# Graph aggregation and routed experts on one core: every engine's turn reordered, and the last two of five epochs joined

## The reference, cut to what matters

```python
# x (12500, 256); src, dst (212500,) with dst sorted; edge_weight (212500,)
def gnn(features, src, dst, w, W, b):
    msgs = features[src] * w[:, None]
    agg = segment_sum(msgs, dst, 12500)
    return agg @ W.T + b
def ffn(xf, ...):                      # 8 experts, D 256, H 512
    probs = softmax(xf @ gate_w + gate_b)
    top2_vals, top2_idx = top_k(probs, 2)
    ...
    # per expert e: y = gelu(xf @ W1[e] + b1[e]) @ W2[e] + b2[e]; out += weight[e] * y
x = x + gnn(layernorm(x), src, dst, edge_weight, W, b)
out = x + ffn(layernorm(x), ...)
```

## Time and profile before

| | |
|---|---|
| median of 3 runs | 2977.66 us (2973.94 to 2983.93) |
| the profiled execution's own time | 2972.63 us |
| its span, first to last instruction | 2970.9 us |
| mean granted clock of PE | 0.869 of full speed |
| busy PE, DVE, ACT, POOL | 74%, 51%, 23%, 62% of the span |
| mean share of the 16 DMA engines | 222 GB/s moved; 41.1% for SP's queue, 27.6% for POOL's |
| gathers | from 3.0 to 2585.4 us |

### The profile page before, as it was taken

The page is one execution under the profiler, slowest core; times in us unless marked ns, Lnnn a source line. Parts: engine busy times, 40 slices in busy tenths (PEclk is TensorE's granted clock), DMA queues, the critical chain, the costliest instruction groups (busy, mean ns, idle before and its releaser), DMA issues.

```text
span 2970.9 us, 47965 instructions
## 1 busy us (share of the span) xinstructions
PE 2196.5 (74%) x11446; PEld 1714.3 (58%) x11447; DVE 1502.6 (51%) x6264; ACT 685.0 (23%) x1950; POOL 1830.6 (62%) x1912
## 2 busy tenths in 40 slices
PE   3666767877777889787787786897887687665585
PEld 2444444665565677565665565676666566554474
DVE  8865454354363554554554544545555363554122
ACT  3411111221221222221221222222222222222131
POOL 6666777767767667767677677675765655500121
PEclk8778879888898999898898898998998888886798
DMA  9654747658568578578698587595976867655674
GB/s 344 231 191 140 234 119 239 212 179 261 193 191 256 189 237 292 173 250 278 198 293 260 167 273 228 181 299 164 297 256 206 262 214 251 180 177 152 208 242 159
DMA packets 306367, 659.36 MB, mean 222 GB/s; under 512 B 61604, under 2 KB 198598, under 8 KB 290342
## 3 DMA queue, kind: packets, MB, share of 16 engines
q1 hardware_dynamic: 213686, 402.45, 41.1%
q0 software_dynamic: 90960, 248.50, 27.6%
q10 hardware_dynamic: 1440, 5.26, 0.5%
HBM read 552.90 MB, written 212.26 MB: 258 GB/s over the span
## 4 chain that ended last, share of the span: by engine, by line
PE 30%; DVE 16%; SPq 16%; POOL 14%; issue 12%; DMA 11%; ACT 1%; DVEq 0%; ACTq 0%; POOLq 0%
POOL rows L383 13%; PE bank L648 9%; SPq L511 9%; PE bank L728 7%; PE bank L741 7%; DMA slots<-stage 4%; SPq L348 3%; DMA w<-in_w 2%; PE bank L680 2%; DVE spread L1037 2%; DMA results<-y_sb,result_i 1%; PE bank L671 1%; DVE item_t L1210 1%; DMA xi<-slots 1%; PE bank L718 1%
## 5 line engine op out<-in xcount | busy, mean ns | idle before, releaser
L383 POOL DMA_INDIRECT rows<-xhat,src_t x1536 | 1476.3, 961 | 522.3 <-issue 460.3
L648 PE MATMUL bank<-rows,spread 128*80 128x256 f32 x3328 | 878.7, 424 | 152.8 <-issue 63.7
L648 PEld LDWEIGHTS bank<-rows,spread 128*80 128x80 f32 x3328 | 552.1, 170 | 423.5 <-issue 197.7
L410 POOL DMA_INDIRECT results<-y_sb,result_i x231 | 229.1, 992 | 520.7 <-DVE y_sb L1243 477.1
L728 PE MATMUL bank<-xiT,w 128*128 128x128 f32 x3696 | 479.2, 285 | 66.0 <-issue 39.0
L728 PEld LDWEIGHTS bank<-xiT,w 128*128 128x128 f32 x3696 | 462.1, 199 | 98.6 <-issue 52.9
L741 PE MATMUL bank<-w,hT 128*128 x1848 | 480.4, 406 | 14.9 <-issue 7.5
L1050 DVE TENSOR_TENSOR acc<-acc,bank 128x160 f32 x208 | 67.0, 322 | 669.9 <-PE bank L638 639.5
L741 PEld LDWEIGHTS bank<-w,hT 128*128 128x128 f32 x1848 | 361.5, 205 | 72.4 <-issue 24.8
L879 ACT ACTIVATE hT<-bank,b1T 128x128 f32<-128x128 f32 x924 | 264.3, 368 | 575.8 <-PE bank L728 572.4
L1037 DVE TENSOR_SCALAR spread<-iota_w,dst_rel,wgt 128x80 f32<-128x80 f32 x1536 | 379.3, 339 | 0.1
(11 more groups left out here) (170 smaller groups left out, 1720.1 us busy)
## 6 DMA issues: line engine op xcount, KB each, us to landing
w<-in_w SPq DMA_DIRECT2D x231, 512.0 KB
slots<-stage SPq DMA_DIRECT2D x784, 136.0 KB
xi<-slots SPq DMA_DIRECT2D x231, 136.0 KB, 4.0
stage<-sorted_x SPq DMA_DIRECT2D x98, 272.0 KB
got<-results SPq DMA_DIRECT2D x97, 256.0 KB
rows<-xhat,src_t POOLq DMA_INDIRECT x1536
x_t<-in_x SPq DMA_DIRECT2D x97, 128.0 KB, 3.1
x_d<-x_t SPq DMA_DIRECT2D x97, 128.0 KB
```

The costliest lines, as they stand in the source:

```text
L383: pool.indirect_dma_start(rows[q][:, c, :], None, x if g < RAW else xhat, bass.IndirectOffsetOnAxis(ap=src_t[:, g * CG + c:g * CG + c + 1] ...
L410: pool.indirect_dma_start(results, bass.IndirectOffsetOnAxis(ap=result_i[i % 2][:], axis=0), y_sb[i % 2][:], None).then_inc(y_out[i % 2], 16)
L648: done = nc.tensor.matmul(B_SUM[0:W, 0:D], spread[g % 2][:, c, :], rows[q][:, c, :], start=c == 0, stop=c == CG - 1)
```

## The change

The plan: a part's softmax, choosing and placing may follow in the turn after the last gate instead of one later, a tile's mask and sort stand in the same turn (after the turn of the place), its copy runs in the turn after it. Results are scattered two turns after their step while edges are gathered. Combined tiles are stored a turn later (`stores`). The last two epochs, of parts (4, 4) and (2, 2, 2), become one of (4, 4, 2, 2, 2): 224 items and 237 turns instead of 231 and 239.

The engines: PE does gate transposition and linear before the down product and sorts after the logits, its second half behind the sums; `rank` goes from the turn of the choosing to that of the placing. The sort gets a PSUM bank of its own, and the up product has one bank instead of two. DVE makes the mask first in a turn. ACT, and not SP, issues the stores of sorted tiles and of residual rows. SP stores outputs and loads items first and copies runs last. Rings: results 2 to 4 (`YB`), output buffers 2 to 6 (`CB`).

```diff
-EPOCH_SIZES = ((6, 8, 8, 8), (8, 8, 8, 8), (8, 6, 4, 4), (4, 4), (2, 2, 2))
+EPOCH_SIZES = ((6, 8, 8, 8), (8, 8, 8, 8), (8, 6, 4, 4), (4, 4, 2, 2, 2))
+YB = 4
+CB = 6
...
-            elif k not in soft_at and gate_at.get(end, tau) < tau:
+            elif k not in soft_at and gate_at.get(end, tau + 1) <= tau:
...
-        if turns:
-            t.sort, t.stage, t.runs = turns[-1].mask, turns[-1].sort, turns[-1].stage
-        if send_next < NT and place_at.get(PART_OF[send_next], tau + 1) <= tau:
-            t.mask = send_next
+        if send_next < NT and place_at.get(PART_OF[send_next], tau) < tau:
+            t.mask = t.sort = send_next
             send_next += 1
+        if turns and turns[-1].sort >= 0:
+            t.stage = turns[-1].sort
...
+        for back in turns if not busy else turns[:-1]:
+            t.results += [s[0] for s in back.steps if s[0] >= 0 and s[0] not in result_at]
         if turns:
-            t.results = [s[0] for s in turns[-1].steps if s[0] >= 0]
-            t.combines = turns[-1].fetches
+            t.combines, t.stores = turns[-1].fetches, turns[-1].combines
...
-        B_SUM, B_TURN, B_XI, B_H0, B_H1, B_Y, B_NODE, B_GATE = [
+        B_SUM, B_TURN, B_XI, B_H, B_SORT, B_Y, B_NODE, B_GATE = [
...
@@ sync turns @@
-                    if t.stage >= 0:
-                        store_sorted(t.stage)
-                    if t.runs >= 0:
-                        copy_runs(t.runs)
...
-                    if t.load_x >= 0:
-                        load_x(t.load_x)
+                    for u in t.stores:
+                        store_out(u)
                     for step in t.steps:
                         if step[3] >= 0:
                             load_xi(step[3])
-                    for u in t.combines:
-                        store_out(u)
                     for u in t.fetches:
                         load_results(u, u in EPOCH_TILES)
-                    if t.linear >= 0:
-                        store_x1(t.linear)
+                    if t.load_x >= 0:
+                        load_x(t.load_x)
                     if t.prep >= 0:
                         store_rows(t.prep)
+                    if t.stage >= 0:
+                        copy_runs(t.stage)
...
@@ tensor: linear, sort, up @@
-                if n_sorted[0]:
-                    pe.wait_ge(sorted_ready, 2 * n_sorted[0])
...
-                pe.wait_ge(x1_ready, n_linear[0])
...
-                if i >= 2:
-                    pe.wait_ge(hT_ready, i - 1)
+                if i:
+                    pe.wait_ge(hT_ready, i)
...
@@ tensor turns @@
                     if t.add >= 0:
                         turn_sums(t.add)
-                    if t.sort >= 0:
-                        sort(t.sort, 0)
                     if t.gate >= 0:
                         turn_node(t.gate)
+                    if t.linear >= 0:
+                        linear(t.linear, fast)
                     for a, _, c, _ in t.steps[:1]:
                         step_down(a, c)
-                    if t.sort >= 0:
-                        sort(t.sort, 1)
-                    if t.linear >= 0:
-                        linear(t.linear, fast)
                     if t.gate >= 0:
                         logits(t.gate)
-                    if t.choose >= 0:
-                        rank(t.choose)
+                    if t.place >= 0:
+                        rank(t.place)
+                    if t.sort >= 0:
+                        sort(t.sort, 0)
                     if t.sums >= 0:
                         sums(t.sums)
+                    if t.sort >= 0:
+                        sort(t.sort, 1)
...
@@ scalar @@
+            def store_sorted(t):
+                if t >= STAGES:
+                    act.wait_ge(runs_in, 16 * NX * (t - STAGES + 1))
+                act.wait_ge(sorted_ready, 2 * t + 2)
+                act.dma_start(stages[t % STAGES][0:2 * P].rearrange("(h p) f -> p h f", p=P), sorted_x[t % 2][:]).then_inc(staged[t % STAGES], 16)
...
+            def store_x1(t):
+                n = valid_rows(t)
+                act.wait_ge(x1_ready, t + 1)
+                act.dma_start(x1_d[t * P:t * P + n, :], x_t[t % XB][0:n, :]).then_inc(x1_out[t % XB], 16)
...
@@ scalar turns: after copy_sums @@
+                    if t.stage >= 0:
+                        copy_sorted(t.stage, 1)
+                        store_sorted(t.stage)
...
+                    if t.choose >= 0:
+                        exponent(t.choose)
                     for _, b, _, _ in t.steps[:1]:
                         if b >= 0:
                             gelu(b)
...
                     if t.linear >= 0:
                         normalise(t.linear)
+                        store_x1(t.linear)
...
@@ vector turns: ahead of add_group; it stood behind place @@
+                    if t.mask >= 0:
+                        mask_choices(t.mask)
...
@@ vector result, and the same in scatter_result @@
-                if i >= 2:
-                    dve.wait_ge(y_out[i % 2], 16 * (i // 2))
+                if i >= YB:
+                    dve.wait_ge(y_out[i % YB], 16 * (i // YB))
```

More of the change, by code:

```diff
@@ L126 @@
     stage: int = -1
-    runs: int = -1
+    stores: list = field(default_factory=list)
     steps: list = field(default_factory=list)
@@ L211, in plan @@
         tau += 1
-        if t.combines and t.combines[-1] == NT - 1:
+        if t.stores and t.stores[-1] == NT - 1:
             return turns
@@ L539, in load_results @@
             def load_results(t, first):
[L540 removed]
+                n, b = valid_rows(t), t % CB
                 if first:
                     last = FIRST_ITEM[EPOCH_OF[PART_OF[t]] + 1]
[L543 to L544 removed]
+                    for q in range(YB):
+                        sp.wait_ge(y_out[q], 16 * len(range(q, last, YB)))
                 sp.wait_ge(x1_out[t % XB], 16 * (t // XB + 1))
[L546 to L547 removed]
+                if t >= CB:
+                    sp.wait_ge(res_out[b], 16 * (t // CB))
                 sp.dma_start(res[b][0:n, :], x1_d[t * P:t * P + n, :]).then_inc(res_in[b], 16)
@@ L751, in turns @@
             def turns(plan, fast):
-                n_linear[0] = n_sorted[0] = 0
                 for t in plan:
@@ L878, in gelu @@
                 for j in range(KH):
-                    done = nc.scalar.activation(hT[i % 2][:, j, :], B_H[i % 2][:, j * P:(j + 1) * P], ACT.Gelu,
+                    done = nc.scalar.activation(hT[i % 2][:, j, :], B_H[:, j * P:(j + 1) * P], ACT.Gelu,
                                                 bias=b1T[:, bass.ds(e * KH + j, 1)])
```

97 lines of the change are left out of this document (36 added, 61 removed).

## The result

The changed kernel takes 2685.97 us (median of 4 runs, 2682.65 to 2688.28), the kernel before 2979.89 (4 runs, 2973.94 to 2983.93): a ratio of 0.9014, 95% interval 0.8994 to 0.9035. The forecast was 2689, in a range of 2630 to 2785. The profiled span went from 2970.9 to 2686.4 us.

What follows compares the result with a forecast made beforehand. POOL was taken to set the pace while edges are gathered, with 227 us of waits to save. Closes -192, tail -72, seven items -31.5 and end +7 gave -288 us: 2684, or 2689 as the runs' median, range 2630 to 2785.

Steps and rivals of the forecast that it cites:

- Closes: Closes of parts while edges are gathered: of POOL's 227 us of waits 35 stay, -192 us (-142 to -222).
- the ring of row buffers: Three row buffers between POOL's gathers and PE's sums: sums may end two gather turns late before POOL feels it.
- Stores to ACT: SP's queue: moving stores to ACT removes its 403.0 us wait for x_t; cover only, no gain counted.
- Mask first, sort in the same turn: DVE's mask and PE's sort in one turn: PE's wait for the mask is hidden, but for 5 us a close.
- One bank for the up product: PE's up product: waiting for the previous item's Gelu costs 0; some 1.2 us an item if cover failed.
- Tail: From the last gather to the last part's items: 212 us become 140, -72 us (-40 to -100).
- Seven items: Last items, where PE alone bounds: the joined epoch has 224 items for 231, at 4.50 us each, -31.5 us.
- End: From the last scatter to the end: seven pairs of tiles at about 3.1 us, 34 us for 27.1, +7.
- PE as the next bound: Gather stretch: PE as near its limit as POOL, lateness adds up at closes, 2775 us; chance 14%.
- Rival 2: The tail keeps its length because its chain is serial, gaining 0 to 20 us: 2750 us; chance 10%.
- Rival 3: Lateness moves from results to sums one for one, and the tail gains 50 us: 2830 us; chance 4%.
- rival 4: Copying on SP becomes the pace, ACT's stores closing a loop, sort turns near 16 us: 3120 us; chance 4%.

Runs made afterwards that it cites:

- Run 5: Kernel before plus four result buffers, scatter two turns after the step, and PE's ranking in the turn of the placing: 2843.26 us, ratio 0.9568.
- run 2: Changed kernel with PE's ranking back in the turn in which DVE chooses: 2790.85 us, ratio 0.9376.
- Run 1: Changed kernel with results scattered one turn after their step, not two, four result buffers kept: 2698.15 us, ratio 0.9056.
- run 4: Kernel before plus only four result buffers and the scatter two turns after the step: 2930.69 us, ratio 0.983.
- Run 7: Changed kernel with the stores of x1 and sorted rows issued by SP again, at the end of its turn ahead of the copies: 2939.18 us, ratio 0.9907.
- Run 6: Changed kernel with DVE making the sort's mask behind its placing, PE's sort still in the same turn: 3040.24 us, ratio 1.0241.
- Run 8: Changed kernel with the old five epochs, 231 items: 2711.97 us, ratio 0.9133.
- run 9: Kernel before with only the last two epochs joined, two pairs of output buffers kept, on a slower chip: 3803.55 us against 3807.85, ratio 0.9993.
- run 3: Changed kernel with two result buffers instead of four, scatter still two turns late: 2908.76 us, ratio 0.9762.

## Why the prediction was right, and where it wasn't

**Closes, -192.** The total is right, but by luck. From 219 to 2396 us POOL has 190 turns and 182 scatters, 190 x 10.02 + 182 x 1.30 = 2140, in 2177 us. What the turns take over their floor went from 228 to 37 us, where I had let 35 stay: -191. The last gather ends at 2396.3 (2390 forecast). The term was written for three edits: ranking, later scatter, four result buffers. Run 5 has just these three in the kernel before, and its last gather ends 119 us earlier, not 192. The step of the prediction that failed is the one from PE's lateness to POOL: I let the ring of row buffers take up the 7 us that PE falls back at a close, and runs 2 and 5 show that most of a wait of PE with sums behind it reaches POOL. The missing 70 us came from the rest of the order, which I had counted as nothing in this stage, so two errors cancel. Within the three edits I gave most to the scatter's extra turn and the buffers. Run 1 gives that turn 12 us in the changed kernel, run 4 turn and buffers together 50 in the old one, but runs 5 and 2 give the ranking 78 to 105.

**Stores to ACT, "no gain of its own".** This step failed too. Run 7 puts 253 us on it, if the stores stand at the end of SP's turn. What they cost at the two places where they stood before, no run shows. By the rule of the Trainium skill that I weighed (DMA: Bandwidth & Descriptors, Issuing engines are not separate DMA queues) another issuer saves issue time alone. The runs agree on the transfers (the same bytes in run 7) and show more on the queue: SP stands 631.7 and 289.2 us at the waits of the two stores, and all its later loads stand behind. I had seen the 403.0 us of the earlier trace rows and called their removal cover.

**Mask first, sort in the same turn, "hidden".** Right as the kernel stands: PE waits 38.9 us at sorts up to the last gather, longest 6.8, where I had said 5 at most for a close. It is more than hidden, since 124.7 us of this wait were there before, and I counted no gain for it. How much of the missing 70 us it makes is open: no run moves mask and sort in the kernel before. Run 6 prices the place of the mask in DVE's list at 354 us, with the sort in the same turn.

**One bank for the up product, 0.** Right so far as the trace shows, though no run gives the second bank back: between an item's transposition and its up no wait for the Gelu appears beyond the 0.52 us of before, and the pitch stayed at 4.49.

**Tail, -72.** From the last gather to the first up of the last items 138.4 us (2396.3 to 2534.7), forecast 140, before 212.6: **-74**. No run aimed at this term, but the traces price some of it, from the last gather to the last scatter, where the changed kernel takes 253.2 us: 12 us more with the ranking back (run 2), 29 more with the mask last (run 6: 281.9), 21 more with the stores on SP (run 7). Of the three edits of run 5 it gets nothing. The six output buffers, which I named first for it, are untested here.

**Seven items, -31.5.** From that up to the last scatter 114.8 us for 145.7: -30.9. Run 8 gives +32.6 when the items come back.

**End, +7.** 36.9 us for 27.1: **+9.8**, a little too small in the forecast. The first load starts 4.6 us after the scatter, and a pair takes 3.7 us in the mean (six from 2657.40 to 2679.67), not 3.1. Runs 8 and 9 bear out its two prices, 3.8 and 6.35 us a pair.

Sum of the measured parts: -191 - 74 - 31 + 10 = -286 us; the spans give -284.5. The sum came out 3 us from the measured time with two of its steps wrong, and that closeness is luck.

**The rivals.** PE as the next bound didn't come: its clock was 0.92 in the gather stage, for 0.88, with 1795 of 2177 us busy for 1839 of 2368, and the dense turns kept up. But PE now waits 121.3 us for gathered rows to land (56.3 in the kernel before), so it does run close behind POOL. Rival 2 is refuted by the 138 us. Rival 3, with its -50, is what run 4 shows for buffers and later scatter alone; with the whole order in place it didn't come. Of rival 4 the mechanism exists, in another place: SP's order is worth 253 us, though ACT's stores don't close the loop.

The prices of single edits don't add up. Taken out one at a time, runs 1, 2, 3, 6, 7 and 8 cost 12 + 105 + 223 + 354 + 253 + 26 = 973 us, against 294 for the whole. The orders of run 6 and 7 are not those of before, and each edit can be what lets another one be free.

## What to carry to other kernels

When one engine's instructions pace the kernel, look for the wait of another engine that its buffers stand behind, and put a turn between that wait and its producer (78 to 105 us here); a later turn for the paced engine's own inputs was worth much less (12). Read every wait in an issuing queue by what is queued behind it and by which turn's work it is for, and not by the bytes: 538 us of waiting for the turn before's tile, behind this turn's item loads, left POOL 24 us of waits up to its last gather, and 632 and 289 us for the same turn's work, ahead of the next item loads, left it 264. Try the edits of a reordering in groups, since a later scatter without its buffers, or a join without its output buffers, gave nothing here, or a loss.

## What the runs showed of the hardware

Two chips timed the kernel before at 2980.29 and 2970.65 us. A third took 3807.85, 28% more, in 17 runs that agree within 1.8%. The instructions of POOL, DVE and ACT last as long there (a gather 960 ns, a mask's halves 0.36 and 0.48 us, a Gelu 369 ns for 368), and once the gathers are over an item takes the same 4.49 us. In the stage with gathers of run 9 PE is granted less clock, 0.80 for 0.88:

```profile
219.00:3417.00 3198.00, 2076.81 (x9512) 1558.05 (x9510) 1196.89 (x4948) 528.92 (x1508) 1641.34 (x1705) 0.80 0.55 166
```

And PE seems to be held for some microseconds at a time. From the waits of ACT and DVE, and from the timeline of one such place, both of run 9:

```profile
ACT xiT L868 <- remote: 493.2, 84, 12.3
```

```profile
1410.54 1.89 PE L741 MATMUL bank<-w,hT 128*128 x8
...
1412.27 0.38 PE L718 MATMUL bank<-ident,xi 128*128 128x128 f32 x2
...
1416.19 0.39 ACT L868 ACTIVATE xiT<-bank 128x256 f32<-128x256 f32 x1 [3.33 <-remote]
1416.33 0.15 DVE L1239 CAST result_i<-xi 128x1 int32 x1 [3.47 <-remote]
```

By its row the transposition ends at 1412.65 and the down product at 1412.43, yet ACT starts on the one at 1416.19 and DVE on the other at 1416.33, 3.5 and 3.9 us later, and both stand idle just before. PE's own next but one product starts at 1418.86. In the kernel before, on its own chip, all 231 copies on ACT start at most 0.04 us after the transposition or ACT's own last work; in run 9, 90 of 224 start over 1 us later, the worst 10.1, 414 us in all, and none in the last 380 us, after the gathers. What holds PE is in no row of the trace. It stays open; a single ratio measured on such a chip says little of the same kernels elsewhere.
